# One audio tower kernel: a number spread by DMA in place of a second normed copy, one norm moved from VectorE to ScalarE, three clears moved to GpSimd, and all five engines in a new order

## The reference

```python
h = frames @ D.T                                   # DCT
h = h + attn(layernorm(h))                         # attention block, then its feed-forward
h = h + ffn(layernorm(h))                          # expert block
# attn(x):  hn = layernorm(x)*ln1_g+ln1_b; q,k,v,g from hn mixed with the token before
#           q, k = exp(rmsnorm(.));  S, Z = decayed linear-attention scan over the tokens, 4 heads
#           x = x + (sigmoid(g) * S/Z) @ Wo.T
#           h2 = layernorm(x)*ln2_g+ln2_b
#           x = x + gelu(h2 @ W1.T) @ W2.T         # the first feed-forward
# ffn(x):   normed = layernorm(x)*ln_g+ln_b
#           x_attn = normed @ attn_w.T + attn_b + x
#           y = gelu(x_attn @ fc1[e].T + b1) @ fc2[e].T + b2     # expert e = batch mod 8
#           out = gelu(y @ next_w.T + next_b)
```

## Time and profile before

| | |
|---|---|
| median of 3 runs | 1095.11 us (1094.64 to 1097.32) |
| the profiled execution | 1096.16 us by its own clock of device time, 1094.2 us span in the trace |
| busy in the span | PE 1058.0 us (97%), DVE 919.4 (84%), ACT 648.0 (59%), POOL 304.8 (28%) |
| DMA queue q1 | 26.7% of 16 engines' span |
| chain that ended last | PE 93%, DVE 4%, ACT 1%, DMA 1% |

### The profile page before, as it was taken

The page is one execution under the profiler, slowest core; times in us unless marked ns, Lnnn a source line. Parts: engine busy times, 40 slices in busy tenths (PEclk is TensorE's granted clock), DMA queues, the critical chain, the costliest instruction groups (busy, mean ns, idle before and its releaser), DMA issues.

```text
span 1094.2 us, 44745 instructions
## 1 busy us (share of the span) xinstructions
PE 1058.0 (97%) x18851; PEld 796.5 (73%) x18851; DVE 919.4 (84%) x2848; ACT 648.0 (59%) x1128; POOL 304.8 (28%) x174
## 2 busy tenths in 40 slices
PE   6679999999999999999999999999999999999997
PEld 6557787786777777777777877777677777777763
DVE  5998988889888888988889898988888888899642
ACT  4346666656765566666566666655576656666533
POOL 4032233242132423313242232324213332331220
PEclk9799999999999999999999999999999999999999
DMA  6232332123323123332212333221332321223210
GB/s 219 88 109 70 97 99 67 53 78 98 98 73 115 54 58 93 97 98 70 83 56 87 98 97 98 71 75 53 97 98 80 102 69 54 89 80 98 80 30 18
DMA packets 51510, 91.55 MB, mean 84 GB/s; under 512 B 9552, under 2 KB 26608, under 8 KB 51312
## 3 DMA queue, kind: packets, MB, share of 16 engines
q1 hardware_dynamic: 51312, 88.69, 26.7%
HBM read 19.50 MB, written 9.78 MB: 27 GB/s over the span
## 4 chain that ended last, share of the span: by engine, by line
PE 93%; DVE 4%; issue 1%; ACT 1%; DMA 1%; SPq 0%; DVEq 0%
PE bank L987 13%; PE bank L1136 11%; PE bank L992 11%; PE bank L1158 10%; PE bank L1129 10%; PE bank L1164 10%; PE bank L1091 7%; PE bank L1066 4%; PE bank L1069 3%; PE bank L1109 3%; PE bank L1074 2%; PE bank L1152 2%; PE bank L1029 2%; PE bank L1113 2%; PE bank L1018 2%
## 5 line engine op out<-in xcount | busy, mean ns | idle before, releaser
L424 POOL TENSOR_TENSOR t_sum<-x,hs 128x512 f32<-128x512 f32 x32 | 40.8, 1276 | 529.9 <-DVE x L795 529.9
L1136 PE MATMUL bank<-w,hid 128*128 128x128 f32 x1024 | 122.7, 278 | 1.5 <-ACT hid L554 1.5
L1158 PE MATMUL bank<-xa,f1w 128*128 128x512 f32 (+1 forms) x256 | 121.1, 570 | 1.9 <-issue 1.8
L574 ACT ACTIVATE hid<-bank,f1b 128x512 f32<-128x512 f32 (+1 forms) x128 | 81.2, 647 | 69.6 <-PE bank L1158 67.7
L1136 PEld LDWEIGHTS bank<-w,hid 128*128 128x128 f32 x1024 | 116.7, 192 | 4.1 <-DVE x L795 1.6
L1129 PE MATMUL bank<-c,w 128*128 128x512 f32 (+1 forms) x256 | 115.8, 565 | 0.9 <-ACT c L548 0.9
L428 POOL TENSOR_TENSOR rr<-vv,nhalf 128x8 f32<-128x8 f32 x32 | 72.3, 2260 | 133.5 <-DVE vv L675 133.5
L1164 PE MATMUL bank<-hid,f2w 128*128 128x512 f32 (+1 forms) x256 | 107.6, 563 | 0.7 <-ACT hid L574 0.7
L1091 PE MATMUL bank<-qx,ki 128*32 128x16 f32 x7680 | 101.0, 193 | 5.7 <-DVE ki L847 5.7
L1091 PEld LDWEIGHTS bank<-qx,ki 128*32 128x32 f32 x7680 | 92.7, 110 | 17.4 <-issue 13.3
L554 ACT ACTIVATE hid<-bank 128x512 f32<-128x512 f32 (+1 forms) x128 | 70.3, 562 | 51.4 <-PE bank L1129 50.4
(11 more groups left out here) (139 smaller groups left out, 2402.9 us busy)
## 6 DMA issues: line engine op xcount, KB each, us to landing
qx<-qq SPq DMA_DIRECT2D x256, 96.0 KB, 2.4
hs<-hs SPq DMA_DIRECT2D x32, 532.0 KB, 3.4
v<-v_f SPq DMA_DIRECT2D x16, 512.0 KB, 3.3
gz<-gate_f SPq DMA_DIRECT2D x16, 512.0 KB, 4.0
xT<-in_xT SPq DMA_DIRECT2D x16, 468.5 KB, 3.5
f1w<-in_fc1T SPq DMA_DIRECT2D x16, 256.0 KB, 3.6
f2w<-g_dram SPq DMA_DIRECT2D x16, 256.0 KB, 3.7
out<-t_sum SPq DMA_DIRECT2D x16, 256.0 KB, 2.4
```

The lines of the kernel that those rows point to most:

```text
L1136: last = mm(dst[:, P * i:P * i + P], hid[:, j, P * m:P * m + P], w2[:, j, :], start=(j == 0), stop=(j == 3))
L1158: mm(dst[:, 0:width[g]], f1w[:, P * j:P * j + P], xa[:, cols(g)], start=True, stop=True).then_inc(f1_ok, 1)
```

## The change

1. **The second copy.** `n2s`, `nmTs` (eight transposes a batch) and the ScalarE `nms` go. VectorE forms for each token the number `ra` = rr3[...,0] * (var+eps) * rr3[...,1] (`ratio`, two small products with a semaphore between). SyncE writes the four columns of `ra` of a group to DRAM as one row of 512 numbers (`hand_ratio`, one number a piece) and reads that row back onto all 128 partitions (`spread_ratio`), into `ra_f`, which is the tile x2. GpSimd multiplies xa by it into c1 (`nms`). The factor f_g goes into a scaled copy of the weights (`wat_g`), f_b into a constant column `at_c`, both made once at the start.
2. **The exchange.** `normed2` goes from VectorE to ScalarE (eight passes of the same form as the `n2s` that went); VectorE computes its offset (`offset2`), one small operation a group.
3. **The clears** of `ko`, `kw` and `ki` are done by GpSimd.
4. **The order** of all five lists and the bank table `USES` are new. A batch's steps from `ats` on now stand at `at(3)`.

```diff
+            def hand_ratio(b, g):
+                used, there = nth(b - 1, 16, 16), nth(b, 2, g + 1)
+                if not first(b):
+                    sp.wait_ge(rb_in[g], used)
+                sp.wait_ge(ra_ok, there)
+                sp.dma_start(ra_dram[g, :].rearrange("(m p) -> p m", p=P), ra[:, four(g)], allow_slow_non_contiguous=True).then_inc(rd_in[g], 16)
+
+            def spread_ratio(b, g):
+                used, there = nth(b - 1, 2, g + 1), nth(b, 16, 16)
+                if not first(b):
+                    sp.wait_ge(nm_ok, used)
+                sp.wait_ge(rd_in[g], there)
+                sp.dma_start(ra_f[:, HALF * g:HALF * g + HALF], ra_dram[g:g + 1, :].to_broadcast([P, HALF])).then_inc(rb_in[g], 16)
...
+            gp.memset(ko[:, :, :], 0.0)
+            gp.memset(kw[:, :, :], 0.0).then_inc(s_lvo, 1)
...
+                if first(b):
+                    gp.memset(ki[:, :, :], 0.0).then_inc(s_lev, 1)
...
+            def nms(b, g):
+                gp.wait_ge(xc_ok, nth(b, 2, g + 1))
+                gp.wait_ge(rb_in[g], nth(b, 16, 16))
+                gp.wait_ge(w1_ok, nth(b, 8, 4 * g + 4))
+                gp.tensor_tensor(c1[:, cols(g)], xa[:, cols(g)], ra_f[:, cols(g)], ALU.mult).then_inc(nm_ok, 1)
...
             def attn_in(b):
                 act.wait_ge(hs2_in, nth(b, 16, 16))
-                before(act, nmT_ok, b, 2, 2)
+                before(act, nm_ok, b, 2, 2)
...
+            def normed2(b, g):
+                act.wait_ge(nb2_ok, nth(b, 2, g + 1))
+                before(act, n1T_ok, b, 2, g + 1)
+                for m in tiles(g):
+                    last = nc.scalar.activation(nl2[:, m, :], x2[:, m, :], ACT.Identity, scale=rr2[:, m:m + 1], bias=nb2[:, m:m + 1])
+                last.then_inc(nl2_ok, 1)
...
-            def n2s(b, g):
-            def nmTs(b, g):
...
+            def ratio(b, g):
+
+                dve.wait_ge(r3_ok, nth(b, 2, g + 1))
+                before(dve, rd_in[g], b, 16, 16)
+                V.tensor_tensor(ra[:, four(g)], rr3[:, four(g), 0], vv3[:, four(g), 0], ALU.mult).then_inc(rm_ok, 1)
+                dve.wait_ge(rm_ok, nth(b, 2, g + 1))
+                V.tensor_tensor(ra[:, four(g)], ra[:, four(g)], rr3[:, four(g), 1], ALU.mult).then_inc(ra_ok, 1)
...
-    [("qT0", 1), ("w1_01", 2), ("kT1", 1), ("w1_13", 2), ("nmT0", 2), ("f1_02", 2), ("nT1", 0), ("f1_10", 2), ("f1_13", 2), ("f2_1", 2)],
+    [("zt", 2), ("rT1", 2), ("wo0", 2), ("k0", 1), ("kT0", 1), ("g0", 1), ("qT1", 1), ("w1_11", 2), ("g1", 1)],
```

More of the change, by code:

```diff
@@ L434, in body @@
                 if (b := at(2)) is not None:
[L435 removed]
+                    pow3(b, 1); nms(b, 1)
                 if (b := at(1)) is not None:
[L437 to L443 removed]
+                    pow2(b, 0)
             every_round(body)
@@ L865, in body @@
             def body(at):
+                if (b := at(2)) is not None:
+                    between(b, 0)
+                if (b := at(3)) is not None:
+                    hidden(b, 0); stats3(b, 0)
+                if (b := at(2)) is not None:
+                    inside(b, 0)
+                if (b := at(3)) is not None:
+                    ratio(b, 0)
+                if (b := at(2)) is not None:
+                    zscan(b); merge(b, 0)
                 if (b := at(1)) is not None:
-                    zmul(b)
+                    stats1(b, 0)
@@ L882, in body @@
+                if (b := at(3)) is not None:
+                    ratio(b, 1); normed3(b, 1)
+                if (b := at(2)) is not None:
+                    merge(b, 2)
                 if (b := at(1)) is not None:
-                    merge(b, 1)
+                    normed(b)
                 if (b := at(2)) is not None:
-                    x_attn(b, 0)
+                    between(b, 1); gate(b, 0); gate(b, 1); merge(b, 3); inside(b, 1)
+                if (b := at(3)) is not None:
+                    x_attn(b, 1)
@@ L1173, in body @@
                 if (b := at(2)) is not None:
-                    pairs_a(b, 6); pairs_b(b, 6); scan(b, 5)
-                if (b := at(1)) is not None:
-                    qkTs(b, 0, 0)
-                if (b := at(2)) is not None:
-                    w1s(b, 0, 0)
-                if (b := at(1)) is not None:
-                    qkTs(b, 1, 0)
+                    zts(b)
+                if (b := at(3)) is not None:
+                    ats(b, 0)
+                if (b := at(2)) is not None:
+                    scan(b, 0); pairs_a(b, 2); pairs_b(b, 2); scan(b, 1)
@@ new lines, in body @@
+                if (b := at(3)) is not None:
+                    f1s(b, 0, 0); f1s(b, 0, 1); f1s(b, 0, 2)
+                if (b := at(2)) is not None:
+                    pairs_a(b, 3); scan(b, 2); pairs_b(b, 3)
+                if (b := at(3)) is not None:
+                    f1s(b, 0, 3)
+                if (b := at(2)) is not None:
+                    rTs(b, 0)
+                if (b := at(1)) is not None:
+                    nTs(b, 0)
+                if (b := at(3)) is not None:
+                    n1Ts(b, 1)
@@ new lines, in body @@
+                if (b := at(1)) is not None:
+                    nTs(b, 1)
+                if (b := at(2)) is not None:
+                    rTs(b, 1)
+                if (b := at(3)) is not None:
+                    f2s(b, 0); ats(b, 1)
+                if (b := at(2)) is not None:
+                    pairs_a(b, 4); scan(b, 3); pairs_b(b, 4); pairs_a(b, 5)
+                if (b := at(3)) is not None:
+                    f1s(b, 1, 0); f1s(b, 1, 1); f1s(b, 1, 2); f1s(b, 1, 3)
+                if (b := at(2)) is not None:
+                    attends(b, 0)
@@ L1181, in body @@
+                if (b := at(2)) is not None:
+                    pairs_b(b, 6); pairs_a(b, 7); n2Ts(b, 0); scan(b, 5); pairs_b(b, 7); w1s(b, 0, 0); w1s(b, 0, 1)
                 if (b := at(3)) is not None:
@@ L1183, in body @@
                 if (b := at(2)) is not None:
-                    pairs_a(b, 7); scan(b, 6); pairs_b(b, 7)
+                    scan(b, 6); scan(b, 7); w1s(b, 0, 2); w1s(b, 0, 3); attends(b, 1)
+                if (b := at(1)) is not None:
+                    qkTs(b, 0, 0); qkTs(b, 1, 0)
+                if (b := at(2)) is not None:
+                    w2s(b, 0)
                 if (b := at(0)) is not None:
@@ L1215, in body @@
-                if (b := at(1)) is not None:
-                    gates(b, 1)
-                if (b := at(2)) is not None:
-                    n1Ts(b, 0); ats(b, 0)
-                if (b := at(1)) is not None:
-                    zts(b); pairs_a(b, 3); scan(b, 1); pairs_b(b, 2)
-                if (b := at(2)) is not None:
-                    f1s(b, 0, 0)
-                if (b := at(1)) is not None:
-                    rTs(b, 0)
-                if (b := at(2)) is not None:
-                    f1s(b, 0, 1)
@@ L1253, in body @@
-                if (b := at(0)) is not None:
-                    qkv(b, "q", 1)
-                if (b := at(2)) is not None:
-                    f1s(b, 1, 3)
-                if (b := at(0)) is not None:
-                    qkv(b, "k", 0); qkv(b, "k", 1)
-                if (b := at(1)) is not None:
-                    scan(b, 4); pairs_a(b, 5); pairs_b(b, 5)
-                if (b := at(2)) is not None:
-                    f2s(b, 1)
-                if (b := at(1)) is not None:
-                    n2Ts(b, 0)
+                    n1Ts(b, 0); w2s(b, 1)
```

359 lines of the change are left out of this document (163 added, 196 removed), and 8 rows, old and new, of the table USES.

## The result

The changed kernel takes 1305.43 us (median of four, 1299.64 to 1308.86) against 1095.3 before in the same job (four runs, 1094.64 to 1097.32): ratio 1.1908, interval [1.1882, 1.1933]. The forecast was 1080, between 1069 and 1099. The profiled execution has a span of 1297.9 us.

A forecast was written before the change was run, and what follows sets the result against it. TensorE sets the pace, 64.7 us a round; latency counts at both ends. Span 1094.2-14.6-5.3+3.0+1.8 = 1079.1, profiled 1081.1, median 1080 us; eight in ten between 1069 and 1099.

The forecast's parts named there:

- I take 3.4, the middle: First DMA of the new route, writing `ra` to DRAM: 3.4 us, between 2.4 and 4.4 of the nearest rows.
- The second DMA: Read of the ratio row back from DRAM, 256 KB: 2.9 us, between ends of 2.4 and 3.7.
- With 0.2 for SyncE: SyncE's share of the route through both DMAs: 0.2 us, making 13.2 us from the end of `w2s(b,1)`.
- the handover by DRAM is too slow: Rival: both DMAs take over 6.3+0.3 us, stopping TensorE each round; at 9 us, 1113 us; chance 0.13.
- The transposes, the exchange and the order: TensorE's transposes gone: -14.6 us; passes exchanged between VectorE and ScalarE: nothing; new order: places had 0.1 to 2 us spare.
- The clears: Clears moved from VectorE to idle GpSimd in the first batch: -5.3 us, bounds 0 and -8.
- other waits of the first batch take over: Rival: in the first batch other waits replace the clears' time: 1085 us, still faster; no chance given.
- +3 for small stops: TensorE's stops each round from late DMAs and other tight places, 0.2 us a round: +3 us.
- +1.8 for the end: Last batch, where nothing covers the route: +1.8 us, between 0 and 5.2.
- The port: Rival: GpSimd's `nms(b,1)` waits for all of VectorE's `inside(b,1)`, about 2 us a round: 1107 us; chance 0.04.
- The signs to watch: Signs of being wrong: rounds above 65 us, TensorE waiting for `pxs` behind `attn_in`, or for `ats(b,1)` on GpSimd's product.
- One sign of being right: TensorE's idle time before `pairs_a`, waiting for px, stays under 3 us in all.

The follow-up runs named there:

- e5: The changed kernel with only the write of the ratio kept; no spread, nobody waits, second norm not computed: 1246.08 us.
- e8: The changed kernel, complete, with the ratio turned by VectorE's 32x32 block transpose and written as 16 pieces of 128 bytes: 1110.25 us.
- e13: e8 with the second group's spread moved ahead of the four loads of `spread(b,2)` in SyncE's list: 1098.64 us.
- e16: The changed kernel with no write; the 256 KB spread reads a row of weights into an unread tile, nobody waits, second norm not computed: 1094.03 us.
- e2: The changed kernel without both DMAs of the ratio; GpSimd multiplies xa by itself, second norm not computed: 1084.37 us.
- e6: e5 with the 512 numbers of a group laid 512 bytes apart in DRAM: 1085.16 us.
- e4: The kernel before with only the three clears moved to GpSimd: 1095.99 us.
- e17: e4 with the clear of `ki` waiting for VectorE's second mix: 1092.21 us.

## Why the prediction was wrong

**The step that failed** is "I take 3.4, the middle" for the first DMA, with 2.4 and 4.4 as its ends, and with it the account that charges a DMA to those alone who wait for it. The write takes 8.5 us and more, outside both ends, and costs 162 us with nobody waiting (e5). The nearest rows, `qx` and `f1b`, write into SBUF; none of them writes to DRAM, and none has pieces that share 64 bytes of it. The prediction said that no row before shows such pieces and bounded them by size all the same. The second DMA was taken at 2.9 and has a median of 4.8 in the page's list, above its upper end too:

```profile
x<-ra_dram SPq DMA_DIRECT2D x32, 256.0 KB, 4.8
```

**Two smaller terms of the route** were short as well, and a quick write alone doesn't save the forecast. "With 0.2 for SyncE" left out that SyncE issues the four `qx` loads between the write and the spread: 2.43 us in e8, where the spread of the second group leaves 3.9 us behind the first write's issue though the writes are quick. Moving it ahead of them brought 1110.3-1098.6 = 11.6 us (e13). And the spread's read was charged to nobody but GpSimd; it costs 9.7 us by itself (e16).

**The rival "the handover by DRAM is too slow"** had the sign and the place (`nms(b,1)`, `attn_in`), if not the step of TensorE. Put 8.7+4.8 = 13.5 us into its own formula, and it gives 1080-3+15 x (13.5-6.6) = 1181. The other 124 us are what no case of mine had: a DMA that slows those who don't wait for it. Of the 221 us over e2, 162 are the write's, waited for by nobody (e5). By the two profiles, after against e2, the span grows by 211.3 us; 69.9 are TensorE's busy time for the same 18725 instructions (1115.0 against 1045.1, at a mean clock of 0.928 against 0.987) and 141.4 its idle time. The two clocks account for nearly all of the 69.9: 1045.1 x 0.987/0.928 = 1111.5. So the stops cost half as much again through the clock that falls behind them.

**The transposes, the exchange and the order** came out as costed, as a sum: no run takes them apart. With the clears' 5.3 us taken back, the sum is 1085.3; the versions without a harmful transfer measured 1084.4, 1084.8 and 1085.2. In e6 `zts` is at 108.6 and at 1002.6 after 14 more rounds, 63.9 us each, against 63.8 forecast. The +3 for small stops and +1.8 for the end were not measured apart; they are right at most as a sum.

**The clears** (-5.3) were worth 0, the lower bound named, as in the rival "other waits of the first batch take over" (1085). Which wait takes over it didn't say: it is VectorE's, shut out by the clear that was moved (e4, e17). The sign set for them, the first `pairs_b` some 5 us earlier, failed too: in the changed kernel it starts at 46.65, 1.3 us later than before. The prediction asked whether GpSimd was idle, not what VectorE does beside it, though it had an instance of the two holding each other up in hand, and of that section of the Trainium skill it weighed only the sentence on two SBUF inputs, for `nms` alone.

**The port** as a rival was not it: in e13, where the product no longer waits for the spread, the 128x426 product of GpSimd takes 1.09 us, in the forecast 1.1 to 1.4.

**The signs to watch** worked: `zts` above 65 us, `attn_in` behind GpSimd's product, TensorE at `ats(b,1)`. The two DMAs "in 6 to 7 us together" failed at once. One sign of being right held all the same: TensorE waited for px before `pairs_a` only 2.5 us in all. The prediction took that for the tightest place, but with the product this late TensorE stops one step earlier, at `ats(b,1)`.

## What to carry to other kernels

A transfer's price is what it does to others as well as when it lands: before a DMA of pieces smaller than the rows at hand goes into a loop, put it there with nobody waiting for it and time the kernel. Don't write 4-byte pieces side by side into DRAM; turn them inside an engine first, or lay them 64 bytes apart. And work given to an idle engine is free only if what the other engine does at that moment doesn't share its access to SBUF.
